# Attention's sums divided by their denominators on GpSimd, two tiles at a time, in place of two turns on TensorE

## What is computed

```python
attn = jax.nn.softmax(jnp.einsum('bhqd,bhkd->bhqk', q, k) * scale, axis=-1)   # 4 heads, d = 16, 320 keys
out = jnp.einsum('bhqk,bhkd->bhqd', attn, v)
out = out.transpose(0, 2, 1, 3).reshape(b, n, c)
out = out @ proj_w + proj_b
return out.transpose(0, 2, 1).reshape(b, c, h, w) + x
```

## Time and profile before

| | |
|---|---|
| median of 3 runs | 11593.28 us (11584.92 to 11602.17) |
| span of the profiled execution, first to last instruction | 11587.8 us (no other time of this execution is recorded) |
| PE busy | 10430.9 us, 90% |
| DVE busy | 8781.7 us, 76% |
| ACT busy | 7244.9 us, 63% |
| POOL busy | 2762.1 us, 24% |

### The profile page before, as it was taken

The page is one execution under the profiler, slowest core; times in us unless marked ns, Lnnn a source line. Parts: engine busy times, 40 slices in busy tenths (PEclk is TensorE's granted clock), DMA queues, the critical chain, the costliest instruction groups (busy, mean ns, idle before and its releaser), DMA issues. The chain is left out here.

```text
span 11587.8 us, 198556 instructions
## 1 busy us (share of the span) xinstructions
PE 10430.9 (90%) x71885; PEld 5268.4 (45%) x72029; DVE 8781.7 (76%) x15079; ACT 7244.9 (63%) x12109; POOL 2762.1 (24%) x5218
## 2 busy tenths in 40 slices
PE   1898998989989899899989989899898998989989
PEld 1544535344453544535445354443534445354453
DVE  6877778777777777778777787777777777777776
ACT  5657566675656757567575666756567565675756
POOL 2312213122131221312223131321312213122130
PEclk9999999999999999999999999999999999999999
DMA  2021220212213022130211302122121221302213
GB/s 61 24 46 47 45 66 25 50 39 51 60 31 59 28 50 56 36 61 34 42 52 42 69 20 47 46 48 63 29 49 35 52 60 31 59 31 49 55 37 74
DMA packets 176570, 537.72 MB, mean 46 GB/s; under 512 B 64872, under 2 KB 87400, under 8 KB 154032
## 3 DMA queue, kind: packets, MB, share of 16 engines
q1 hardware_dynamic: 175664, 525.31, 20.1%
HBM read 232.49 MB, written 71.30 MB: 26 GB/s over the span
## 5 line engine op out<-in xcount | busy, mean ns | idle before, releaser
L978 DVE TENSOR_REDUCE R<-ps 128x2 f32<-128x640 f32 x4096 | 3182.3, 817 | 889.4 <-PE ps L714 888.1
L1185 ACT ACTIVATE R<-ps 128x512 f32<-128x512 f32 x5120 | 2819.2, 594 | 646.8 <-PE ps L735 621.6
L258 ACT ACTIVATE R<-R,st 128x1475 bf16<-128x1475 f32 (+1 forms) x1326 | 2077.1, 1566 | 489.9 <-DVE st L330 465.1
L319 DVE TENSOR_SCALAR_CACHE_REDUCE R<-R,st 128x1255 bf16<-128x1255 f32 (+1 forms) x1326 | 1936.4, 1460 | 18.6 <-DVE st L330 0.2
L714 PE MATMUL ps<-KST,R 96*128 96x320 bf16 x8192 | 1802.2, 301 | 40.6 <-DVE R L978 31.0
L760 PE MATMUL ps<-R 128*32 128x512 f32 x12288 | 1638.8, 606 | 38.0 <-DVE Wk L931 32.8
L735 PE MATMUL ps<-R,KST 104*128 104x512 bf16 x4096 | 1563.0, 384 | 38.6 <-ACT R L1185 23.1
L714 PEld LDWEIGHTS ps<-KST,R 96*128 96x128 bf16 x8192 | 754.3, 98 | 727.4 <-DVE R L978 215.1
L1268 POOL CAST R<-Wk 128x512 bf16<-128x512 f32 x256 | 283.7, 1108 | 2477.3 <-DVE Wk L931 2477.3
L735 PEld LDWEIGHTS ps<-R,KST 104*128 104x128 bf16 x4096 | 394.2, 97 | 724.4 <-ACT R L1185 458.6
L384 POOL TENSOR_TENSOR R<-R,sB 128x1024 f32<-128x1024 f32 x136 | 255.1, 1897 | 1642.7 <-DMA R<-xh_in 1637.3
(11 more groups left out here) (210 smaller groups left out, 19138.3 us busy)
## 6 DMA issues: line engine op xcount, KB each, us to landing
R<-R SPq DMA_DIRECT2D x3072, 64.0 KB, 2.4
R<-xh_in SPq DMA_DIRECT2D x136, 512.0 KB, 4.5
out_dram<-Z SPq DMA_DIRECT2D x68, 1024.0 KB, 3.9
R<-xa_in SPq DMA_DIRECT2D x36, 1024.0 KB, 11.4
R<-xb_in SPq DMA_DIRECT2D x36, 1024.0 KB, 12.0
R<-sr_in SPq DMA_DIRECT2D x32, 1024.0 KB, 5.4
R<-sr_in SPq DMA_DIRECT2D x16, 2016.0 KB, 9.2
R<-sr_in SPq DMA_DIRECT2D x16, 1056.0 KB
```

The source lines that it names most:

```text
L258: e.activation(junka[:, 0:o2 - o1], xc[:, o1:o2], ACT.Sign, bias=mid, scale=-1.0, accum_out=ca[i]).then_inc(md_ca, 1)
L319: e.tensor_scalar(junk[:, 0:o1 - o0], xc[:, o0:o1], mid, None, ALU.is_le, ALU.add, accum_out=cv[i]).then_inc(md_cv, 1)
L978: e.tensor_reduce(MX[(4 * u + s4) % 2][:, blk_, h0:h0 + 2], ps[:, 2 + 2 * bq:4 + 2 * bq, 0:320], axis=AX.X, op=ALU.max).then_inc(mx, 1)
L1185: e.activation(PB[:, t % 2, w, :], ps[:, w % 2, :], ACT.Exp).then_inc(ex, 1)
```

## The change

- The columns of values and ones that `weigh` multiplies by are interleaved: of the 128 rows of bank 7, and so of `OR`, the even ones are sums and the odd ones denominators.
- SP issues two DMAs for each tile (`lay_out`). They take the even rows of `OR` to 64 partitions of `XO` and the odd rows to the same 64 partitions of `XD`: the first 64 for an even tile, the other 64 for an odd one.
- For each pair of tiles POOL runs `normalise(q)`: an approximate reciprocal of `XD` from its bits (one `tensor_scalar` on an int32 view), three Newton steps of three instructions, and a multiplication by `XO` into `ON`. These are 11 instructions on 128 x 512 fp32, each of which waits for the one before.
- PE projects two tiles at once (`project_out(q)`, four matmuls, step 2 of tile `2q+4`), and DVE adds 128 x 512 to `Z` at once. The transposes, the reciprocals, the multiplication on DVE and the copy on ACT are gone. The loop has three rounds after the last tile in place of two.

```diff
-        ON = W[:, 1024:1280]
-        OX = W[:, 1280:1536]
+        XO, XD, XI, ON = W[:, 1024:1536], R2[:, 1024:1536], R2[:, 1536:2048], R2[:, 2048:2560]
...
+        def lay_out(e, t):
+            h0 = 64 * (t % 2)
+            src = OR[t % 2]
+            row = src.ap[0][0]
+            e.wait_ge(ou, t + 1)
+            if t > 1:
+                e.wait_ge(on, t // 2)
+            for k, dst in enumerate((XO, XD)):
+                e.dma_start(dst[h0:h0 + 64, :], bass.AP(src.tensor, src.offset + k * row, [[2 * row, 64], [1, 512]])
+                            ).then_inc(in_o[t % 2], 16)
... (PE)
-            def denominators(t):
-                e.wait_ge(ou, t + 1)
+            def project_out(q):
+                e.wait_ge(on, q + 1)
                 e.wait_ge(*b6[0])
                 for i in range(4):
-                    op = e.transpose(ps[:, 6, 128 * i:128 * i + 128], OR[t % 2][:, 128 * i:128 * i + 128], c("ident"))
-                op.then_inc(den_ps, 1)
-                b6[0] = (on, t + 1)
-
-            def turn_back(t):
...
-            def project_out(t):
-                e.wait_ge(ox, t + 1)
-                for i in range(2):
-                    op = e.matmul(ps[:, 6, 128 * i:128 * i + 128], lhsT=OX[:, 128 * i:128 * i + 128], rhs=c("pw"),
+                    op = e.matmul(ps[:, 6, 128 * i:128 * i + 128], lhsT=ON[:, 128 * i:128 * i + 128], rhs=c("pw"),
                                   start=True, stop=True)
                 op.then_inc(po_ps, 1)
-                b6[0] = (zo, t + 1)
+                b6[0] = (zo, q + 1)
...
-            for t in range(NT + 2):
+            for t in range(NT + 3):
...
-                    if w in (4, 6) and t == NT + 1:
-                        busy(0, w // 2)
-                    if w == 4 and done2:
-                        turn_back(t - 2)
-                    if w == 6 and done2:
-                        project_out(t - 2)
-                    if w == 9 and prev:
-                        denominators(t - 1)
+                    if w < 6 and t == NT + 1:
+                        busy(0, 2)
+                    if w == 2 and t > 3 and t % 2 == 0:
+                        project_out(t // 2 - 2)
... (DVE)
-            def denominators(t):
-                heads = ps[:, 6, :].rearrange("p (a d) -> p a d", a=16)
-                e.wait_ge(den_ps, t + 1)
-                e.reciprocal(RD[t % 2], heads[:, :, 16]).then_inc(rc, 1)
...
-            def project_out(t):
-                u, s4 = t // 4, t % 4
+            def project_out(q):
+                u, s4 = q // 2, 2 * (q % 2)
                 w0 = 2 * (16 * (u // 2) + 4 * s4) + u % 2
-                zo_ = Z[:, :, w0:w0 + 7:2]
+                zo_ = Z[:, :, w0:w0 + 15:2].rearrange("p c (b i) -> p c b i", b=2)
...
+                    if w == 4 and t > 3 and t % 2 == 0:
+                        project_out(t // 2 - 2)
... (ACT)
                     if w == 8 and prev:
                         e.wait_ge(pv_ps, t)
                         if t > 2:
-                            e.wait_ge(den_ps, t - 2)
+                            e.wait_ge(in_o[(t - 1) % 2], 32 * ((t - 1) // 2))
                         e.activation(OR[(t - 1) % 2], ps[:, 7, :], ACT.Copy).then_inc(ou, 1)
...
-                        e.activation(OX, ps[:, 6, 0:256], ACT.Copy).then_inc(ox, 1)
... (POOL)
+            def normalise(q):
+                for half in range(2):
+                    e.wait_ge(in_o[half], 32 * (q + 1))
+                if q:
+                    e.wait_ge(po_ps, q)
+                n = 10 * q
+                e.tensor_scalar(XI.bitcast(I32), XD.bitcast(I32), -1.0, NEAR, ALU.mult, ALU.add).then_inc(nt, 1)
+                for _ in range(3):
+                    e.wait_ge(nt, n + 1)
+                    e.tensor_tensor(ON, XD, XI, ALU.mult).then_inc(nt, 1)
+                    e.wait_ge(nt, n + 2)
+                    e.tensor_scalar(ON, ON, -1.0, 2.0, ALU.mult, ALU.add).then_inc(nt, 1)
+                    e.wait_ge(nt, n + 3)
+                    e.tensor_tensor(XI, ON, XI, ALU.mult).then_inc(nt, 1)
+                    n += 3
+                e.wait_ge(nt, n + 1)
+                e.tensor_tensor(ON, XO, XI, ALU.mult).then_inc(on, 1)
...
+                    if w == 4 and t > 2 and t % 2:
+                        normalise(t // 2 - 1)
... (SP)
+                if t:
+                    lay_out(e, t - 1)
+            lay_out(e, NT - 1)
...
-            e.wait_ge(zo, NT)
+            e.wait_ge(zo, NT // 2)
```

More of the change, by code:

```diff
@@ L9 @@
 BF16 = mybir.dt.bfloat16
+I32 = mybir.dt.int32
 ALU = mybir.AluOpType
@@ L36 @@
 BIG = 2.0 ** 100
+NEAR = float(0x7EF311C7)
 SMALL = {}
@@ L991, in values @@
                 e.wait_ge(va_ps, 1)
-                e.memset(VX[:, 0:8, 16:32], 1.0)
+                e.memset(VX[:, 0:8, 1::2], 1.0)
                 e.memset(VX[:, 8:12, :], 0.0)
-                e.memset(VX[:, 0:8, 0:16], 0.0).then_inc(vm, 1)
+                e.memset(VX[:, 0:8, 0::2], 0.0).then_inc(vm, 1)
                 e.wait_ge(vm, 1)
                 for r in range(2):
-                    op = e.memset(VX[64 * r:64 * r + 64, 8 + r:12:2, 16:32], 1.0)
+                    op = e.memset(VX[64 * r:64 * r + 64, 8 + r:12:2, 1::2], 1.0)
                 op.then_inc(vm, 1)
@@ L1000, in values @@
                 for i in range(2):
[L1001 removed]
+                    e.tensor_copy(VX[:, 4 * i:4 * i + 4, 0::2], ps[:, 7, 64 * i:64 * i + 64].rearrange("p (h d) -> p h d", h=4))
                 for r in range(2):
[L1003 removed]
+                    op = e.tensor_copy(VX[64 * r:64 * r + 64, 8 + r:12:2, 0::2],
                                        ps[64 * r:64 * r + 64, 7, 128:192].rearrange("p (h d) -> p h d", h=4)[:, r::2, :])
                 op.then_inc(vx, 1)
[L1007 to L1018 removed]
+            def project_out(q):
+                u, s4 = q // 2, 2 * (q % 2)
                 w0 = 2 * (16 * (u // 2) + 4 * s4) + u % 2
[L1020 to L1022 removed]
+                zo_ = Z[:, :, w0:w0 + 15:2].rearrange("p c (b i) -> p c b i", b=2)
+                e.wait_ge(po_ps, q + 1)
+                if q == 0:
                     e.wait_ge(zb, 4)
[L1024 removed]
+                e.tensor_tensor(zo_, ps[:, 6, :].rearrange("p (i b c) -> p c b i", i=4, b=2), zo_, ALU.add).then_inc(zo, 1)
             for t in range(AHEAD):
@@ L1029, in vector @@
                 split_max(t)
-            for t in range(NT + 2):
+            for t in range(NT + 3):
                 u, s4, ahead = t // 4, t % 4, t + AHEAD
-                live, prev, done2 = t < NT, 0 <= t - 1 < NT, t >= 2
+                live = t < NT
                 for w in range(10):
-                    if w == 0 and done2:
-                        denominators(t - 2)
-                    if w == 7 and done2:
-                        project_out(t - 2)
+                    if w == 4 and t > 3 and t % 2 == 0:
+                        project_out(t // 2 - 2)
                     if w < 8 and live and ahead < NT:
@@ L1187, in scalar @@
                         lay_max(t + AHEAD - 1)
-                    if w == 4 and t >= 2:
-                        e.wait_ge(ot_ps, t - 1)
-                        if t > 2:
-                            e.wait_ge(po_ps, t - 2)
-                        e.activation(OX, ps[:, 6, 0:256], ACT.Copy).then_inc(ox, 1)
                     if (t, w) in STAGES:
```

21 lines of the change are left out of this document (4 added, 17 removed), and 4 rows, old and new, of the table SIGNALS.

## The result

The changed kernel takes 13016.09 us (median of 4 runs, 13005.56 to 13028.82) against 11597.17 for the kernel before on the same chip: 1.1226 times as long, 95% interval 1.1212 to 1.1241. The forecast was 13400, its range 12350 to 14150.

The account below looks back on a forecast made before the run. PE bounds the tile loop; the prediction had it wait for POOL, closing a loop A + D + N of 24.2 us a pair for 19.6. With clock loss and the image's end, +113.8 us an image, +1805 in all: 13400 us, range 12350 to 14150.

Parts of the forecast that it names:

- A: From a pair's projection on PE to the end of the next pair's OR copy: 6.1 us, 8.1 with clock loss.
- D: From the end of the OR copy, through SP's DMAs, to the start of `normalise` on POOL: 3.3 us.
- N: POOL's 11 instructions of `normalise` for a pair: 14.8 us, from 10.0 to 16.0.
- the first rival: POOL's four `tensor_scalar` take 0.61 us each, so N = 12.1: 12710 us, down to 12250; chance 0.15.
- four `tensor_scalar` at 1.26 us: In `normalise` on POOL: 512 in a row priced from other shapes' rows; four take 5.0 us (2.4 to 6.2).
- the saving on PE: Per pair, from the turns, the wait at the next scores and two projections becoming one: 0.97 us.
- I count 0.15 there: PE's saving per tile from dropping `denominators`, since the next scores also wait for the exp of step 8.
- The clock: Some 4 us behind each PE stall run at the lower clock: A loses 2.0 us; bounds 0 and 3.5.
- The stall: PE idle before each pair's projection: D + N of 18.1 against 12.5 us of work, so 5.6 us.
- Stage pairs: Four pairs of an image with an even tile's stage first on POOL: 1.6 us late each, 6.4 together.
- The case of a faster kernel: Rival: with N at most 9.2 the chain is hidden in the loop; net -6 us per image, 11500 us; chance 0.03.
- the third rival: POOL's instructions dearer still, 0.3 us more for each of the 11: +845, 14240 us; chance 0.08.

Follow-up runs that it names:

- e9: The kernel before with 18 `tensor_scalar` of different shapes, scalars and operation counts on POOL ahead of the first image: 11607.48 us, a single run.
- e12: The changed kernel with the three `tensor_scalar` of the Newton steps multiplying only, without the addition, so the result is no reciprocal: 13801.93 us.
- e1: The changed kernel with two Newton steps in place of three, so a less exact reciprocal: 11892.5 us.
- e3: The changed kernel with twelve matmuls without use on PE ahead of the projection's wait for POOL: 12751.08 us.
- e8: The kernel before without the transposes of `turn_back` and the ACT copy behind them, so its output is not the attention's: 11436.48 us.
- e4: The changed kernel with the projection of a pair one tile later, at step 2 of tile `2q+5`: 12442.31 us.
- e7: The changed kernel, projection at step 9, a pair's lay-outs together, last pair normalised on VectorE, next image's first-half load behind the lay-out: 11706.64 us.
- e10: As e7, but the last two pairs are normalised on VectorE and SP's lay-outs go ahead of the parts of queries: 11653.49 us.
- e11: As e10, but every pair is normalised on VectorE, in four pieces of 128 columns at steps 5 to 8 of the odd tile: 12626.19 us.

## Why the prediction was right, and where its sum was off

The mechanism held: PE waits for POOL in every pair, the loop A + D + N closes and sets the time, the wait costs clock as well, and the image's end lies open. The number owes something to luck: 13400 is near 13016 because errors of opposite sign were added. With the right N and its other terms as they stand, the prediction's sum is the first rival's 12710, 306 too low. Point by point:

- **The failed term: four `tensor_scalar` at 1.26 us.** They take 0.62, so N is 12.2 and not 14.8, 2.6 less in each of 16 pairs, 41.6 us an image. The step that failed is "with 2.0 ns for an element and 12 ns for a row these agree". It fitted three rows by their shapes, and did not look at what they computed: L1283 has one operation, the change's have two (e9, e12). For one operation the fit was too low as well, 1.26 for 1.46 to 1.50. The first rival had N = 12.1 right, but not the time. The Trainium skill (GPSIMD Engine Reference, "Engine selection") says that one input runs at about line rate there. The 0.61 and 0.62 of this form agree; the 1.46 and 1.50 of the form with one operation do not.
- **It was offset by 18 us an image on the other side.** Against the values of the prediction: D 3.52 for 3.3, +3.5 in all; pair 13, whose lay-out lands behind the next image's 2 MB (D 7.9), +4.4; pair 1, behind twelve loads on SP, +0.8; A, +5.9; the leg at tile 32, 6.3 for 4.6, +1.7; the last projection at half clock and its addition, 2.8 for 1.8, +1.0; PE's start 0.05 behind POOL, +0.8. Net -23.5: +88.7 us an image, where +112.8 were forecast, and 16 times that is the difference of the two spans. Had N been 14.8, the kernel would have taken 13802 (e12) and not 13400.
- **A and the saving on PE.** At full clock A is 6.76 (e1, e3). "I count 0.15 there", for the wait at step 0, was too much: without `denominators` PE waits 0.74 there for the exp, as long as the 0.17 and 0.58 of before together, so that removing it gave nothing back. The projection takes a slot of 0.99 us (12666.70 to 12667.69), not 0.75. The turns did come off the path (e8), but the steps in which they and the old projection stood now wait for VectorE's reductions instead: three in a row take 2.29 us. This last is read from the rows, not tested. The pair bound by PE is 19.76 for 18.6.
- **The clock.** 2.0 us a pair predicted, 1.6 measured in a plain pair (e3). The granted clock over the whole attention of an image is 0.91, where "under 0.9" was named as a sign. And the sign "24 if the clock holds" deceives: the pairs are 24.1 us apart although the clock falls, because N is shorter.
- **The stall** is 2.7 us where 5.6 were forecast: 2.6 less from N, 0.5 less since PE has 13.0 us of work before it comes to the wait and not 12.5, and 0.2 more from D.
- **Stage pairs.** D is 5.19 where a stage stands ahead, +1.67; predicted 1.6.
- **The case of a faster kernel.** The prediction put the turning point at N near 9.6. e1, with N = 8.8, is still 2.5% slower without the wait in plain pairs, since PE gets nothing back and the end lies open. So there is no turning point near 9.6 in this order; a still shorter N was not run.
- **The dearer GpSimd** (the third rival) did not come: N is 12.1 to 12.2 in every pair, with VectorE busy beside it, and the int32 view costs what fp32 does (0.62).
- **Not foreseen:** that SP's queue, which "has most of a tile to spare" in the prediction, closes a second loop through the single `XO` and `XD` (e4), which a longer lead of the projection does not open.

## What to carry to other kernels

When work leaves a bound engine for an idle one, find the loop: what must come back before the next round of the same work can begin, and whether that sum is longer than the round; then look at every queue it passes, since the one that waits longest hides the next. Take a price from a row with the same operations, not from one with the same shape alone. And look at where nothing runs behind the chain: here the loop could be mended to 19.03 us for 19.59, but each image's end, 3.7 us before, stayed at 10.4 at best.

## What the runs showed of the hardware

- `tensor_scalar` on GpSimd, 128 x 512 fp32 with numbers: multiply and add 0.61 to 0.62 us (on int32 too, L1253), multiply alone 1.46 to 1.50 (e9, e12). 64 x 256 with multiply alone: 0.84, and 0.92 with a scalar from SBUF, whether the row is flat or 16 rows of 16.
- VectorE's `reciprocal` on 128 x 512 from SBUF takes 3.35 us (e7, e10), on 128 x 128 0.94 (e11); a product of 128 x 512 takes 0.69 there and 1.26 on GpSimd.
- A lay-out of 128 KB that lands in 2.8 us takes 7.5 when 2 MB were issued ahead of it (pair 13 of the changed kernel).
- TensorE fell to its lower clock behind one idle spell of 2.7 us in each pair (0.55 in the 3 us behind), and in e11 among and behind several waits of under 1 us each (0.77 in 6 us in which it was busy for 3.15, then 0.60); matmuls without use ahead of the wait kept it at full clock (e3).
